# Cross-attention over eight batches: two PSUM banks in turn for the head outputs, one for the scores whose maxima are taken

## The reference

```python
# layer 0, of which only batch 0 of the attention is used
q, k, v = heads(x @ Wq.T), heads(ctx @ Wk.T), heads(ctx @ Wv.T)
att = softmax(q @ k.T / sqrt(32)) @ v
x = x + att[0]
# layer 1
xq, ykv = layer_norm(x, gq, bq), layer_norm(ctx, gkv, bkv)
q = heads(xq @ Wq);  k, v = heads(ykv @ Wkv)
o = softmax(q @ k.T / sqrt(32)) @ v
x = x + o @ Wproj + bproj
h = gelu(layer_norm(x, gm, bm) @ W1 + b1)
x = x + h @ W2 + b2
```

## Time and profile before

| what | us |
|---|---|
| median of 3 runs | 1885.43 |
| lowest and highest run | 1879.63, 1895.04 |
| the profiled execution, whole | 1889.92 |
| its span, first to last instruction | 1888.1 |
| TensorE busy (matmuls) | 1750.5 |
| ScalarE busy | 1166.9 |
| VectorE busy | 1094.3 |
| GpSimd busy | 935.6 |
| granted TensorE clock, mean share | 0.972 |

### The profile page before, as it was taken

One profiled execution on the slowest core, in us unless ns is written; L12 is line 12 of the kernel. 1 busy time (PEld: TensorE's weight loads), 2 busy tenths in 40 slices (PEclk: granted clock), 3 DMA queues, 4 the chain that ended last, 5 costly groups with the idle time before them and its releaser, 6 DMA issues.

```text
span 1888.1 us, 23894 instructions
## 1 busy us (share of the span) xinstructions
PE 1750.5 (93%) x7488; PEld 1339.1 (71%) x7488; DVE 1094.3 (58%) x1860; ACT 1166.9 (62%) x1935; POOL 935.6 (50%) x778
## 2 busy tenths in 40 slices
PE   6899999887898899999999999999999999999898
PEld 5677777655566677767667767777776677677687
DVE  4566655565676565756655655656566666654322
ACT  3677774677777666756756576667566565765231
POOL 0455422476764464546544554655455455546331
PEclk8999999999999999999999999999999999999999
DMA  6689945787545664675466455646654774557262
GB/s 231 220 286 294 310 173 177 270 276 237 183 125 176 162 185 132 189 201 165 141 201 182 143 157 172 197 126 186 205 160 138 211 187 143 157 168 243 81 237 89
DMA packets 156382, 354.69 MB, mean 188 GB/s; under 512 B 28512, under 2 KB 47072, under 8 KB 155360
## 3 DMA queue, kind: packets, MB, share of 16 engines
q1 hardware_dynamic: 125440, 240.95, 41.8%
q10 hardware_dynamic: 30816, 112.21, 19.1%
HBM read 251.51 MB, written 82.08 MB: 177 GB/s over the span
## 4 chain that ended last, share of the span: by engine, by line
PE 69%; ACT 8%; DVE 6%; DMA 6%; issue 5%; POOL 3%; SPq 3%; DVEq 0%; ACTq 0%; POOLq 0%
PE ps_d L862 46%; PE ps_o L911 11%; PE ps_t L894 5%; PE ps_s L879 5%; DMA q_st<-negmax_t 3%; SPq L637 2%; DVE negmax L1147 1%; ACT ps_d L927 1%; DMA k_st<-k_scratch 1%; PE ps_d L792 1%; DVE rs_t L1126 1%; ACT p_hi L1006 1%; ACT ps_t L1013 1%; ACT L1006 1%; DVE stats L1104 1%
## 5 line engine op out<-in xcount | busy, mean ns | idle before, releaser
L1257 POOL TENSOR_TENSOR p_lo<-p_full,p_hi 128x512 fp32r<-128x512 f32 x288 | 371.5, 1290 | 633.9 <-ACT p_full L1013 631.2
L1006 ACT ACTIVATE p_hi<-ps_t 128x512 fp32r<-128x512 f32 x576 | 345.2, 599 | 417.0 <-PE ps_t L894 416.1
L1147 DVE TENSOR_REDUCE negmax<-ps_s 128x1 fp32r<-128x512 f32 x576 | 389.9, 680 | 187.5 <-PE ps_s L879 187.2
L862 PE MATMUL ps_d<-hT,w_r 128*128 128x512 f32 x1536 | 432.3, 398 | 3.5 <-DVE hT L1052 1.8
L862 PE MATMUL ps_d<-w_r,g_s 128*128 128x512 f32 x1536 | 399.7, 398 | 5.5 <-DMA w_r<-w_scratch 5.5
L862 PEld LDWEIGHTS ps_d<-hT,w_r 128*128 128x128 f32 x1536 | 293.0, 191 | 81.7 <-DVE hT L1052 3.0
L862 PEld LDWEIGHTS ps_d<-w_r,g_s 128*128 128x128 f32 x1536 | 294.6, 192 | 77.2 <-issue 8.7
L1160 DVE TENSOR_TENSOR p_lo<-ps_t,p_hi 128x512 fp32r<-128x512 f32 x288 | 198.7, 690 | 231.4 <-ACT ps_t L1013 229.8
L911 PE MATMUL ps_o<-p_hi,v_s 128*65 128x512 f32 x576 | 236.6, 411 | 45.9 <-ACT o_raw L1029 40.9
L894 PE MATMUL ps_t<-q_st,k_st 97*128 97x512 f32 x576 | 235.8, 409 | 32.3 <-DMA q_st<-negmax_t 32.2
L879 PE MATMUL ps_s<-k_st,q_st 96*128 96x512 f32 x576 | 236.8, 411 | 11.3 <-DVE negmax L1147 9.6
(11 more groups left out here) (99 smaller groups left out, 2185.1 us busy)
## 6 DMA issues: line engine op xcount, KB each, us to landing
w_r<-w_scratch ACTq DMA_DIRECT2D x214, 512.0 KB, 5.1
w_r<-w_scratch SPq DMA_DIRECT2D x42, 512.0 KB, 4.7
v_scratch<-v_out SPq DMA_DIRECT2D x36, 520.0 KB, 3.9
v_s<-v_scratch SPq DMA_DIRECT2D x36, 520.0 KB, 5.2
k_scratch<-kq_out SPq DMA_DIRECT2D x36, 512.0 KB, 3.9
q_scratch<-kq_out SPq DMA_DIRECT2D x36, 512.0 KB, 3.3
q_st<-q_scratch SPq DMA_DIRECT2D x144, 128.0 KB, 4.3
k_st<-k_scratch SPq DMA_DIRECT2D x144, 128.0 KB, 4.3
```

The lines of the kernel that those rows point to most:

```text
L862: ins = nc.tensor.matmul(bank(u), lhs[a], rhs[b], start=(i == 0 and m == 0), stop=(i == 3 and m == 2))
L1006: act.activation(p_hi[:, c], ps_t[:, c % 2], ACT.Exp, scale=SCALE)
L1147: dve.tensor_reduce(negmax[:, h % 2, c:c + 1], ps_s[:, c % 2], AX.X, ALU.max, negate=True).then_inc(s_maxed, 1)
L1257: pool.tensor_tensor(p_lo[:, c], p_full[:, (by_gpsimd(s) - 1) % 2], p_hi[:, c].bitcast(F32), ALU.subtract).then_inc(p_pool_split, 1)
```

## The change

The eight banks are shared out anew. `ps_o` gets two, used in turn by even and odd heads, and `ps_s` keeps one. The waits follow: a score matmul waits for the maximum of the chunk just before it, and the first output matmul of a head waits for the move of the output before the last. No instruction is added, removed or placed elsewhere.

```diff
-    ps_s = nc.alloc_psum_tensor("ps_s", [P, 2, T], F32)
+    ps_s = nc.alloc_psum_tensor("ps_s", [P, T], F32)
     ps_t = nc.alloc_psum_tensor("ps_t", [P, 2, T], F32)
-    ps_o = nc.alloc_psum_tensor("ps_o", [P, T], F32)
+    ps_o = nc.alloc_psum_tensor("ps_o", [P, 2, T], F32)
...
-                if s >= 2:
-                    pe.wait_ge(s_maxed, s - 1)
-                nc.tensor.matmul(ps_s[:, c % 2], q_st[0:KQ, h % G, c * P:c * P + P], k_st[0:KQ, h % G],
+                if s:
+                    pe.wait_ge(s_maxed, s)
+                nc.tensor.matmul(ps_s[:], q_st[0:KQ, h % G, c * P:c * P + P], k_st[0:KQ, h % G],
                                  start=True, stop=True).then_inc(s_ready, 1)
...
                 if c == 0:
-                    if h:
-                        pe.wait_ge(o_moved, h)
+                    if h >= 2:
+                        pe.wait_ge(o_moved, h - 1)
...
-                    ins = nc.tensor.matmul(ps_o[0:VW], v_s[:, group % 2, c, h % G], src[:, c],
+                    ins = nc.tensor.matmul(ps_o[0:VW, h % 2], v_s[:, group % 2, c, h % G], src[:, c],
...
-                act.activation(o_raw[0:VW, h % 2], ps_o[0:VW], ACT.Identity).then_inc(o_moved, 1)
+                act.activation(o_raw[0:VW, h % 2], ps_o[0:VW, h % 2], ACT.Identity).then_inc(o_moved, 1)
...
-                dve.tensor_reduce(negmax[:, h % 2, c:c + 1], ps_s[:, c % 2], AX.X, ALU.max,
+                dve.tensor_reduce(negmax[:, h % 2, c:c + 1], ps_s[:], AX.X, ALU.max,
                                   negate=True).then_inc(s_maxed, 1)
```

## The result

The changed kernel takes 1910.99 us (median of 6 executions), the kernel before took 1890.62 us (6) on the same chip. The ratio is 1.011, with a 95% interval of 1.007 to 1.015: slower by 20 us. The profiled execution took 1910.9 us, its span is 1909.1.

The account below looks back on a forecast made before the run. TensorE's own stream was taken to bound the kernel (busy 1750.5 of 1888.1 us). Terms 9 + 2.5 + 5 - 4 gave +12.5 us on the profiled 1889.9 us, so 1902.4 us; range 1881 to 1918.

Parts of the forecast that it names:

- start to batch 1: First attention, 45 to 300 us: about 1 us hidden at its start, delays at two later inversions; +2.5 us.
- batches 1 and 2: Dense attentions where VectorE comes late; +5 us for both, ends -13 and +61.
- batches 3 to 8: Six attentions repeating one pattern, worked out on the fourth batch: 1.5 us each, 9 us in all.
- the clock: Half clock behind TensorE's waits: -4 us, ends -21 and +10; as rival, all 21 us return, 1878, chance 0.08.
- The output wait: TensorE's wait for ScalarE's move of a finished head output, 40.9 us in 26 waits; predicted to go near 0.
- the burst: Ticks 24 to 26, around a whole group's Gelu: of 2.87 us of removed wait, 0.71 us is left as gain.
- the inversion: Ticks 29 and 30, VectorE inverting a group's row sums: score matmul 0.57 us later, +0.28 us left with the burst's 0.71 spent.
- the row wait: At tick 51 TensorE waits 3.32 us for the row of maxima, made late by an earlier store; predicted 1 us shorter.
- the cover of tick 46: The 0.96 us delay at ticks 46 and 47 costs nothing, absorbed by the 3.32 us row wait at tick 51.
- clusters: Groups of shortfalls in batches 1 and 2; the first delay takes up most later ones, 1 to 2.3 us stays of each.
- shortfalls: Amounts by which score matmuls start before the previous chunk's maximum is done: 109 cases, 110 us, hidden by two banks.
- The slower rival: VectorE's lateness feeds itself in the dense batches, row waits move along; some 30 us stay, +37 in all, 1922; chance 0.30.

Follow-up runs that it names:

- e8: e4 (two dense banks, two score banks) with two output banks in place of one; 1936.11 us, ratio to before 1.0250.
- e9: e7 with VectorE taking the next tick's maximum ahead of p_lo at ticks 24 and 40, from the fourth attention on; 1859.63 us, ratio to before 0.9867.
- e3: Changed kernel, with the spare bank as second score bank in the first three attentions, second output bank in the six behind; 1893.24 us, ratio to before 1.0037.
- e10: e7 with the spare bank switched from scores to outputs after the first attention in place of the third; 1885.64 us, ratio to before 0.9995.
- e1: Changed kernel with one output bank as before, so only the score bank is taken away; 1916.28 us, ratio to before 1.0153.
- e4: Kernel before with two banks for the dense parts in place of three; 1952.42 us, ratio to before 1.0339.
- e7: e3's bank switch after three attentions together with e6's late spread of the inversions; 1871.11 us, ratio to before 0.9912.
- e6: Kernel before with row-sum inversions spread over four ticks, only from the fourth attention on; 1885.45 us, ratio to before 0.9980.
- e2: Changed kernel with VectorE's row-sum inversion steps over four ticks in place of two, GpSimd's joins one or two ticks later; 1891.41 us, ratio to before 1.0020.

## Why the prediction was right, and where it was off

The forecast was +12.5 us on the kernel before; measured was +20, inside the range, on the side that was forecast. The mechanism was right, and the sizes were not: at full clock every term was too small, and the clock gave back three times what was forecast. That the total came out as near as it did is partly luck.

The two profiles, stage by stage, between the first score matmuls of the attentions. "At full clock" is the length times the granted clock of the stage, so it counts half clock as if TensorE had been busy all through it, an estimate.

| stage | forecast | measured | measured, at full clock |
|---|---|---|---|
| start to batch 1 | +2.5 | +7.6 | +5.9 |
| batches 1 and 2 | +5 | +7.4 | +12.5 |
| batches 3 to 8 | +9 | +5.4 | +13.9 |
| behind the last score matmul | 0 | +0.5 | +0.5 |
| the clock | -4 | in the stages | -12 |
| all | +12.5 | +21 | +21 |

**The output wait is gone and most of it comes back one station later.** Right. Forecast for the burst: a removed wait of 2.87 us leaves 0.71. In the profiles the distance from the score matmul of tick 25 to that of tick 26 fell from 5.75 (916.78 to 922.53) to 4.60 us in batch 4, 1.15 less. e8 and e9 show the cause from two other sides: with two score banks, or with the maximum taken early, TensorE stops at the transposed matmul for a late p_lo.

**Batches 3 to 8: +9 us, before the clock's share.** The places are right, the sum too small. e3 measures +7 us (3 to 12) for them, but with the clock's share in it. The distances between score matmuls of one batch, changed kernel less kernel before, as a mean of the six batches (of five for the last row); stretches that are left out changed by less than 0.1 us:

| ticks | forecast | measured | at full clock |
|---|---|---|---|
| 12 to 24 | +0.43 | +0.57 | +0.57 |
| 24 to 28, the burst | -0.71 | -1.18 | -0.32 |
| 28 to 32, the inversion | +0.99 | +1.19 | +1.19 |
| 40 to 43 | -0.30 | -0.30 | -0.30 |
| 43 to 46 | +0.96 | +0.94 | +0.94 |
| 46 to 52, with the row wait | -0.96 | -0.73 | -0.82 |
| 52 to 61 | 0 | -0.63 | +0.03 |
| 61 to the next batch | +1.08 | +0.94 | +0.94 |

Two steps were off most: the burst gave 0.3 us at full clock where 0.7 was forecast, and the inversion cost 0.2 more. The others stand near the forecast, the cover of tick 46 among them (3.32 to 1.66 at tick 51). The forecast took every wait at its own length and left out the 0.1 us behind each.

**The first attention: +2.5 us.** Too small. Its stretch with the projections behind it, to the first score matmul of batch 1, ends at 353.9, 350.7 and 349.5 us in the three profiles with one score bank there, and at 344.8 to 349.1 in the seven with two score and three dense banks: 4 us on average.

**Batches 1 and 2: +5 us.** Wrong in size, and the term that was furthest off. The two profiles show 12.5 us at full clock, e10 measures 16. The clusters were rightly found, and the cover too: the row waits absorbed 10 us of batch 1. But the forecast counted two reliefs against the same shortfalls, the first delay of a cluster and the row waits behind it, and left almost nothing. In batch 1 VectorE is late against more than every third score matmul: 24 waits where the view had 5. Of the shortfalls of 61 us a fifth to a quarter stays, not a twelfth. That TensorE is held again at once behind each cover is my reading of these counts; no run tests it apart. The slower rival had this place and this direction, with half of the shortfalls left over and a total of 1922; its own mechanism, row waits that move along and cover nothing, is not what happened. Its sign was growth of over 15 us in these two batches: the two profiles show 7.4, and e10's 16, give or take 6, doesn't decide it.

**The clock: -4 us.** Too small. The kernel before was granted 0.972 in its profile and, over the 19 and 23 executions timed beside the first eight experiments, 0.972 on average; the changed kernel 0.979, in its profile and on average. The part not granted is 0.028 of 1888 = 53 us before and 0.021 of 1909 = 40 us after, -12 to -13 us. That is the high end, as TensorE is idle in part of it: it was busy for 95 us at half clock before and for 75 after, half of which makes -10. The forecast had looked only at the six later batches, 21 of the 53 us. Of the 12 us, 5 came back beside the bursts of these batches, 3 in the rest of them and 3 ahead of them. At tick 26 half clock still follows the shorter wait in five of the six. In batch 3 a wait of 2.12 us ends at 761.33, and this is the window behind it (columns as above, clock 0.51):

```profile
762.00:765.40 3.40, 3.40 (x10) 2.44 (x9) 1.25 (x2) 1.62 (x3) 3.25 (x3) 0.51 0.51 144
```

Why there is less half clock in all, no run shows.

The stage numbers of e3 and e10 contain their part of the clock and don't add to it; with e10's 16, e3's 7 and the 4 us of the first attention the sum is 27, 7 above the measured 20, which the intervals of e3 and e10 (4 and 6 us) cover.

**Two rules of the Trainium skill.** The Trainium skill's page "PSUM — Partial Sum Buffer", section "Summary: rules for kernel authors", wants a different bank for the matmul than the one that is read. e1 agrees: the score bank alone costs 1.5%, 29 us, far below the 426 us of the case in which every matmul stands right behind the last. The Trainium skill's page "TensorE: Matmul & The Clock Gate", section "HAM oscillation — how this bites in real kernels", tells of one kernel in which double buffering gave no further gain. Here it gave 17 us (e8 against e4) and 13 us (e7 against e6), so the runs decide against carrying it over.

What stays open: which of VectorE's producers makes it late in batches 1 and 2. In the largest case the norm's statistics stand ahead of the maximum; that wasn't tried apart.

## What to carry to other kernels

A second buffer removes the wait at its own station, and what the stream gains is the distance to the next thing that is late for the same reason: look that one up in the trace before counting the wait as gain. A bank taken away costs where its reader is late, and this is found by laying each writer beside the end of the reader before it, not by the reader's share of time; in a dense stretch take the sum of the shortfalls seriously even if idle time behind them seems to cover it. Often the lateness can be moved for less than a bank: here the order of a few small VectorE steps took 0.9% off the changed kernel (e2) and 0.45% off e7 (e9). Together with giving the bank back to the scores in the first three attentions (e3, e7), a loss of 1.1% became a gain of 1.3%.

## What the runs showed of the hardware that I had not expected

The copy of the inversion takes its time from GpSimd. It ends 0.27 to 0.29 us after the GpSimd instruction that started before it, here in three cases: 943.10 + 1.29 = 944.39 and 943.11 + 1.55 = 944.66 in the changed kernel (rows above); the same in the kernel before, 934.19 after 933.91 (copy in the earlier trace rows, first fence), and in e2, 948.43 after 948.14 (second fence):

```profile
932.63 1.28 POOL L1265 TENSOR_TENSOR g_s<-h_st,g_s 128x512 fp32r<-128x512 f32 x1 [0.91 <-ACT g_s L1022]
```

```profile
946.85 1.29 POOL L1265 TENSOR_TENSOR g_s<-h_st,g_s 128x512 fp32r<-128x512 f32 x1 [0.92 <-ACT g_s L1022]
```

The whole trace of the changed kernel has 36 such copies. 26 of them start while a GpSimd instruction is under way, and each ends 0.28 or 0.29 us after it; the other ten take some 0.42 us. On average the copy took 1.04 us in the kernel before and 0.73 in e2, the same instruction at another place. This is as the Trainium skill's page "SBUF — State Buffer", section "Who interferes with whom", has it: a copy of VectorE that uses the port pair shared with GpSimd waits until a GpSimd instruction that came first has ended. The trace agrees.

And the clock's share differs between kernels with the same work, and steadily enough to be compared as a mean of several executions: 0.967 to 0.977 in all executions of the kernel before, 0.980 or 0.981 in all five of e9. A single profile is too little for it: in the changed kernel it ranges from 0.974 to 0.981.
